# Pairing the steps of attention from step 4 instead of step 6 in the first batch, with the blocks of keys and queries and their spreads in another order

## What is computed

```python
xn = layernorm(x)
q, k, v = xn @ w_q.T, xn @ w_k.T, xn @ w_v.T          # 16 heads of 16 channels
weights = softmax(q @ k.T * 0.25)                     # per head, 1024 queries x 1024 keys
x = x + layernorm((weights @ v) @ w_o.T)
xn2 = layernorm(x); prev = shift_by_one_token(xn2)
xr, xk = mix(xn2, prev, mu_r), mix(xn2, prev, mu_k)
r = sigmoid(xr @ W_r.T); act = relu(xk @ W_k.T) ** 2
out = x + layernorm(r * (act @ W_v.T))
```

## Time and profile before

| | |
|---|---|
| median of 3 runs | 1205.41 us (1203.61 to 1206.33) |
| the profiled execution | 1205.2 us |
| its span, first to last instruction | 1203.4 us |
| PE busy | 1185.4 us, 99% of the span |
| ACT busy | 1058.6 us, 88% |
| DVE busy | 779.3 us, 65% |
| POOL busy | 271.2 us, 23% |

### The profile page before, as it was taken

One profiled execution on the slowest core, in us unless ns is written; L12 is line 12 of the kernel. 1 busy time (PEld: TensorE's weight loads), 2 busy tenths in 40 slices (PEclk: granted clock), 3 DMA queues, 4 the chain that ended last, 5 costly groups with the idle time before them and its releaser, 6 DMA issues.

```text
span 1203.4 us, 25781 instructions
## 1 busy us (share of the span) xinstructions
PE 1185.4 (99%) x10594; PEld 654.8 (54%) x10594; DVE 779.3 (65%) x1840; ACT 1058.6 (88%) x1419; POOL 271.2 (23%) x337
## 2 busy tenths in 40 slices
PE   9999999999999999999999999999999999999997
PEld 6544555555555555455554555555554555535455
DVE  6644757757675765947577575767668466554656
ACT  6789898998989989898988989899898989989882
POOL 3000222222221322222122222213222122222132
PEclk9999999999999999999999999999999999999999
DMA  5455664217513294315744176221852149400100
GB/s 175 121 164 156 119 123 92 90 54 155 110 54 89 78 171 89 85 39 129 137 76 119 53 137 112 72 89 54 174 109 56 35 104 160 90 1 19 54 19 18
DMA packets 61960, 113.78 MB, mean 95 GB/s; under 512 B 6544, under 2 KB 31376, under 8 KB 61648
## 3 DMA queue, kind: packets, MB, share of 16 engines
q1 hardware_dynamic: 61248, 110.39, 40.3%
q10 hardware_dynamic: 560, 1.31, 0.3%
HBM read 69.47 MB, written 41.94 MB: 93 GB/s over the span
## 4 chain that ended last, share of the span: by engine, by line
PE 95%; ACT 2%; DVE 1%; DMA 1%; issue 0%; POOL 0%; SPq 0%; POOLq 0%; DVEq 0%
PE O L549 39%; PE M L531 28%; PE M L486 23%; PE M L428 3%; ACT PT L726 2%; PE M L659 1%; PE M L456 1%; DMA mu<-w_dram 1%; DVE sth L942 0%; PE M L652 0%; PE M L636 0%; ACT KS L749 0%; ACT xA L796 0%; PE M L594 0%; DVE xB L1077 0%
## 5 line engine op out<-in xcount | busy, mean ns | idle before, releaser
L726 ACT ACTIVATE PT<-M 128x512 f32<-128x512 f32 (+1 forms) x1277 | 1000.2, 864 | 108.0 <-PE M L531 97.1
L531 PE MATMUL M<-QS,KS 50*128 50x512 f32 x2048 | 499.5, 419 | 7.8 <-ACT PT L726 7.8
L549 PE MATMUL O<-PT,V 128*17 128x512 f32 x4096 | 490.5, 596 | 0.0
L531 PEld LDWEIGHTS M<-QS,KS 50*128 50x128 f32 x2048 | 222.0, 185 | 261.6 <-ACT PT L726 235.2
L549 PEld LDWEIGHTS O<-PT,V 128*17 128x17 f32 x4096 | 93.7, 96 | 229.3 <-issue 210.7
L486 PE MATMUL M<-xnT,WH 64*128 64x512 f32 x504 | 148.7, 408 | 0.0
L1341 POOL TENSOR_SCALAR veh<-mvh 128x2 f32<-128x2 f32 x90 | 20.0, 222 | 404.2 <-DVE mvh L945 404.2
L1184 DVE SCALAR_TENSOR_TENSOR A<-Z,M 128x512 f32<-128x512 f32 x30 | 20.6, 688 | 109.2 <-PE M L486 109.2
L486 PE MATMUL M<-WH,xnT 64*128 64x256 f32 x480 | 85.1, 285 | 0.0
L486 PE MATMUL M<-WH,C 64*128 64x256 f32 x480 | 84.1, 285 | 0.0
L486 PE MATMUL M<-WH,B 64*128 64x256 f32 x480 | 83.9, 285 | 0.0
(11 more groups left out here) (166 smaller groups left out, 1695.0 us busy)
## 6 DMA issues: line engine op xcount, KB each, us to landing
scr<-p SPq DMA_DIRECT2D x124, 256.0 KB
QS<-scr SPq DMA_DIRECT2D x56, 256.0 KB, 6.8
KS<-scr SPq DMA_DIRECT2D x56, 256.0 KB, 9.4
QS<-scr SPq DMA_DIRECT2D x70, 128.0 KB, 5.7
KS<-scr SPq DMA_DIRECT2D x68, 128.0 KB, 7.5
xB<-x_dram SPq DMA_DIRECT2D x16, 512.0 KB, 6.9
xA<-x_dram SPq DMA_DIRECT2D x15, 512.0 KB, 6.9
out_dram<-xB SPq DMA_DIRECT2D x15, 512.0 KB, 4.4
```

Source lines behind the costliest of these rows:

```text
L531: e.matmul(PM[bank[i, j]], KS[qd][rows, pair, kt * 128:kt * 128 + 128], QS[qd][rows, pair, hf * 512:hf * 512 + 512], start=True, stop=True) \
L549: ins = e.matmul(PO[32 * j:32 * j + 17, :], V[b % 2][:, kt, 4 * qd + j, :], PT[i % 3][:, j, :], start=(kt == 0), stop=(kt == 7))
L726: e.activation(PT[i % 3][:, j:k + 1, :], PB[:, at:at + len(numbers), :], ACT.Exp, scale=SCALE) \
```

## The change

`PAIRED` goes from 6 to 4, so steps 4 and 5 are computed by `period(4)`. The pieces of the first batch move: K10 goes ahead of Q10, and Q10, K11, Q01 and Q11 each begin two or four steps later. The spreads move with them. One semaphore more is used for them, and waits that name the last reader of a half of `xnT` name Q10 instead of K10.

```diff
-PAIRED = 6
+PAIRED = 4
...
-FIRST = {0: "K00", 1: "V2", 2: "K01", 3: "V3", 4: "Q10", 5: "K10", 6: "K11", 8: "Q01", 10: "Q11", 12: "T0", 18: "T1",
+FIRST = {0: "K00", 1: "V2", 2: "K01", 3: "V3", 4: "K10", 6: "Q10", 8: "K11", 10: "Q01", 12: "T0", 14: "Q11", 18: "T1",
...
-SENT = ("Q00", "K00", "K01", "Q10", "K10", "K11", "Q01", "Q11")
+SENT = ("Q00", "K00", "K01", "K10", "Q10", "K11", "Q01", "Q11")
...
-FIRST_SPREADS = {1: [(1, (0,), (0,))], 2: [(1, (1,), (0,))], 5: [(1, (1,), (1,))], 6: [(2, (0,), (0,))], 7: [(2, (1,), (0,))],
-                 9: [(2, (1,), (1,))], 10: [(3, (0, 1), (0,))], 11: [(3, (1,), (1,))],
-                 16: [(qd, (0,), (1,)) for qd in range(4)]}
+FIRST_SPREADS = {1: [(1, (0,), (0,))], 2: [(1, (1,), (0,))], 4: [(1, (1,), (1,))], 8: [(2, (1,), (0,)), (3, (1,), (0,))],
+                 10: [(2, (0,), (0,))], 11: [(3, (0,), (0,))], 12: [(2, (1,), (1,))], 13: [(3, (1,), (1,))],
+                 18: [(qd, (0,), (1,)) for qd in range(4)]}
...
-        batch = 0 if i < 12 else owner(word, u)
+        batch = 0 if i < 18 else owner(word, u)
...
-        first_in = [sem(f"first_in{i}") for i in range(12)]
+        first_in = [sem(f"first_in{i}") for i in range(13)]
...
-                        p.wait_ge(("piece", piece), ("piece", ((("K10", "Q11"), ("V1", "V3"))[b > 1][g], b - 1)))
+                        p.wait_ge(("piece", piece), ("piece", ((("Q10", "Q11"), ("V1", "V3"))[b > 1][g], b - 1)))
...
-                    p.wait_ge(("bank", piece), ("piece", ((("K10", "Q11"), ("V1", "V3"))[b > 1][g], b - 1)))
+                    p.wait_ge(("bank", piece), ("piece", ((("Q10", "Q11"), ("V1", "V3"))[b > 1][g], b - 1)))
```

## The result

The changed kernel takes 1210.06 us (median of 6 runs, 1208.74 to 1213.05) where the kernel before takes 1204.73 (6 runs, 1203.42 to 1206.33). The ratio is 1.0050, with a 95% interval of 1.0039 to 1.0061: slower by 5.3 us, clear of the 0.2% that the prediction set as the least that can be told. The forecast was 1212.5 in a range of 1207.8 to 1218.0. The profiled execution took 1209.97 us, with a span of 1208.2 us.

A forecast was written before the change was run, and what follows sets the result against it. The prediction took PE to bound the kernel (95% of 1203.4 us). A net +5.7 us from the wait at score (17, 1) plus 1.6 for the clock gave +7.3 on 1205.2: 1212.5 us, range 1207.8 to 1218.0.

The forecast's parts named there:

- the likeliest case: PE waits at score (17, 1) and its clock falls behind that: +7.3 us, 1212.5 us, chance 0.58.
- Part 1: Steps 4 and 5 as a pair instead of two single steps: PE gains 1.70 us until quad 2.
- Part 2: SP's chain from K01's store to Q10's spread: PE waits 7.4 us at score (17, 1), net +5.7 us.
- the landings: On SP, from the end of a store's issue to the spread waiting for it: 4.8 us, ends 4.3 and 5.2.
- the eight DMAs: On SP, eight DMAs instead of four issued ahead of Q10's store: 4.6 us (3.5 to 6.7).
- Rival 3: SP's chain runs at its shortest: +2.2 us, with the clock +3.8, 1207.4 to 1209 us; chance 0.08.
- however much PE gains ahead of it: At score (17, 1): net stays 5.7 us, since the chain starts from K01's store, which the pairing doesn't move.
- the shortest row at each place: Lower end of SP's chain to score (17, 1): Q10's spread landed at 70.5, 2.2 us above before.
- Part 3: PE's clock falls to 1.2 GHz behind the wait at score (17, 1): 1.6 us lost, ends 0 and 3.1.
- The other spreads: K11's spread, due at score (21, 1), has slack of 1.4 to 3.0 us: cost 0, upper end 2 us.
- the half piece in steps 16 and 17: Half a piece more in the pair of steps 16 and 17, hidden behind ACT's exponentials: 0 to 0.01 us.
- Rival 4: Stores land early and Q10 is there before score (17, 1): the 1.70 us stay, 1203.5 us; chance 0.06.

The follow-up runs named there:

- experiment 8: experiment 5 with K11's spread to quad 2 moved to step 11 and the q spread for quad 3 to step 12: 1203.47 us, ratio 0.9988.
- experiment 9: experiment 8 with PAIRED = 6 again, so steps 4 and 5 are single: 1204.69 us, ratio 1.0003.
- experiment 11: experiment 8 with T1 moved from step 18 to 20, exchanged with Q00: 1201.83 us, ratio 0.9984.
- experiment 4: Changed kernel with PAIRED = 6 again and all its tables kept, so steps 4 and 5 are single: 1210.35 us, ratio 1.0042.
- experiment 2: Changed kernel with only the k spread for quad 3 moved, from step 8 to step 11: 1209.91 us, ratio 1.0048.
- experiment 3: Changed kernel with 18 added products of 128x512 ahead of score (17, 1), keeping PE busy over the wait: 1209.45 us, ratio 1.0040.
- experiment 7: Changed kernel with Q10 and K10 exchanged in pieces, stores and spreads, so Q10 goes first: 1208.86 us, ratio 1.0041.
- experiment 1: Changed kernel with step 8's k spreads moved behind Q10's store, quad 2's to step 9, quad 3's to step 10: 1208.33 us, ratio 1.0032.
- experiment 5: experiment 1 with the k spread for quad 3 moved from step 10 to 11, behind K11's store: 1207.91 us, ratio 1.0030.
- experiment 6: experiment 5 with PAIRED = 6 again, so steps 4 and 5 are single: 1207.91 us, ratio 1.0031.
- experiment 10: experiment 5 with the first load of xB (512 KB) at step 17 instead of 12: 1204.57 us, ratio 1.0005.

## Why the prediction was right, and where its terms were off

The time lay in the range, and the likeliest case was the right one. But its sum had two wrong sizes, 3.1 us too much for the chain on SP and 1.4 too little for the clock, and one term of 0.5 was missing. That they partly offset each other, so that the total was off by 2 us and not by more, is luck.

**Part 1, the pairing.** Right: 5.61 us for the first pair, 4.38 for the next (5.64 and 4.43 forecast), the fuller pair of steps 16 and 17 at +0.01. Experiments 8 and 9 show its worth once no spread is late: 1.57 us in the trace, 1.2 in the medians; in the trace of experiment 11, where PE waits for DVE no more either, it is 1.74 against the kernel before.

**Part 2, Q10's way to quad 2.** The wait was there, at the place named, ended by the DMA named, and anchored on K01's store nearly as said (experiment 4 moved it by 0.7 us). Its size was too large: 4.24 us, not 7.4; net +2.6, not +5.7. All of the terms but the last came out near their lower ends. K01's spread began 4.3 us behind its store and took 1.71 (4.7 and 2.50 forecast), the landings took 4.30 and 4.10 (4.8 each, with 4.3 as the lower end), the eight DMAs 3.87 (4.6). The last one, from the first issue of Q10's spread to the score, took 4.72 (4.8). I had taken the mean of six groups of four, three of which were held up while being issued; here only the last group was. Rival 3, the short chain, I gave 0.08, because I thought it unlikely that six terms come out low together. Five did, and not only once: in the traces of experiments 2, 3, 4 and 7 the landings of K10's and Q10's stores took 3.9 to 4.6 us, and K01's spread took 1.71 in all eight experiments with pairs from step 4. With pairs from step 6 it never did (experiment 4), so that term was low by the pairing itself and not by luck, and the sentence that the net is the same "however much PE gains ahead of it" fails by about 0.7 us. The kernel before had 4.3 to 5.2 for a landing; why it was slower there no run tells. The prediction's two ends of this part were also not quite what it calls them: "the shortest row at each place" has 2.9 for the last landing, where the earlier trace rows have 2.6 for a q spread, and the lower end of the range, 1207.8, is given as rival 3 without the clock, which by its own terms is 1207.4. Neither changes the forecast.

The figure of the Trainium skill (DMA: Bandwidth & Descriptors, Latency and other measured facts), about 2 us for a DMA, would have put the net at +0.1. Measured is +2.6, so it would have missed by 2.5, and my 4.8 missed by 3.1: the net alone doesn't decide between them, since my other terms were too long. The landings themselves do, with 4.30 and 4.10 they are nearer to 4.8 than to 2. And a net of +0.1 would have said that the kernel stays as it is.

**Part 3, the clock.** The mechanism was right, the size was not: 3.0 us, not 1.6, close to the upper end of 3.1 that I gave. I had taken the price from the fall at 31 us, where the slow stretch was half as long. The clock fell in all seven profiles with a wait of 2.6 us or more (the changed kernel, experiments 1, 2 and 4 to 7), and not in experiment 3, in which PE worked over the wait, nor behind the waits of 0.37, 0.71 and 1.33 us in experiments 3 and 10. What it costs depends on how much of the slow stretch lies behind the wait: with 5.03 us of waiting in experiment 7, where the clock fell between 66 and 67 us and PE went on at 70.00, the rest of the pair took 5.3 us; in the changed kernel, where it fell at about 69 and PE went on at 69.49, it took 6.65; at 2.4 GHz it takes 3.65. And the fall at 31 us, which I took as a fixed part of the kernel's head, comes in only three of the thirteen profiles.

**What I missed.** The pair of steps 18 and 19 grew by 0.52 us. Q11 now ends two steps later, so DVE takes it out at 78.49 to 79.90 and serves quad 1's outputs behind it until 82.4, and takes T1 out last; PE waits 0.46 us for the bank (`DVE On L967`). Before, DVE was idle for 0.54 us ahead of T1. I had said that the half piece in steps 16 and 17 costs nothing, and looked at PE and ACT for that, not at DVE, which has to take every piece out. Experiment 11 removed that wait.

**The other spreads.** I gave (21, 1) 1.4 to 3.0 us of slack. In the changed kernel it held, but only because the slow clock had delayed PE: with the clock kept up, experiment 3 waited 1.33 us there. So "cost 0" was right for the changed kernel by way of the very clock term that was too small.

**Rival 4**, that the spread would be in time and 1.7 us gained, had the right price: with an order that makes it true, the trace of experiment 8 gives 1.18 us, less by the wait for DVE, and that of experiment 11 gives 1.74 (0.65 and 1.82 between the medians).

## What to carry to other kernels

Before you move work earlier on the bounding engine, follow each of its later consumers of DMAs back along the issuing queue to the first event that the change doesn't move: if that chain has no slack, next to nothing of the gain is left however large it looks (0.6 of 1.7 us here), and most of any step added to the chain is paid. Repair such a chain consumer by consumer, in the order in which they are due, and once the order is right look at the transfers ahead of the one that is waited for: a load of 512 KB that nobody needed soon cost about 2 us here. And add to a wait of PE of a few microseconds what the slow clock behind it costs, 1.6 to 3 us here.

## What the runs showed of the hardware

- In waits of PE of 2.6 to 5.0 us, or up to 1 us behind their end (experiments 5 and 6), the granted clock fell to 0.50 (1.2 GHz) and stayed there for a while with PE at work again; in the changed kernel that cost 3.0 us behind a wait of 4.2. Eighteen products over the same time kept it at 1.00.
- Pauses of 0.30 and 0.41 or 0.42 us at 28 to 31 us stand in all thirteen profiles. In three (the kernel before, experiments 3 and 8) the clock fell behind them, in the others not, with the same instructions. A difference of 1.5 us between two executions can be that alone; it has to be taken out before two traces are compared.
- A DMA of a spread landed 2.2 to 4.1 us after its issue in the kernel before, at a DMA share of 0.3 to 0.6. At a share of about 1.0 to 1.15 K11's spread took 3.7 to 5.3 us in the changed kernel and 5.2 to 7.1 in experiment 5. Taking one load of 512 KB out from in front of it gave about 2 us back at the consumer (experiment 10).
- A store's two parts of 256 KB each needed 3.9 to 5.7 us from the end of their issue to the spread that waited for them, over all kernels; the longest was K11's in experiment 1, with a spread and the load of `xB` issued in between.
- The time that SP takes to issue four DMAs of a spread is not fixed: 1.71 to 3.75 us, and for K01's it went with PE's steps (1.71 with pairs from step 4, 1.94 to 2.83 with pairs from step 6).
